# Mixture of experts: the sum over eight experts by identity matmuls on TensorE instead of reductions on VectorE

## The reference, cut to what matters

```
for e in range(E):                                   # E = 8 experts, 64 channels, 128 hidden
    h = gelu(einsum('bsd,dh->bsh', xn, W1[e]) + b1[e])
    y_e = einsum('bsh,hd->bsd', h, W2[e]) + b2[e]
    y = y + y_e * w_full[..., e, None]               # weights: softmax of the two largest logits, else 0
h = h + y
```

## Time and profile before

| | us |
|---|---|
| median of 3 runs (1759.25 to 1766.6) | 1764.92 |
| the profiled execution, its own time | 1765.77 |
| its span, first to last instruction | 1764.0 |
| TensorE busy | 1532.9 (87%) |
| VectorE busy | 1243.7 (71%) |
| ScalarE busy | 719.1 (41%) |
| POOL busy | 635.5 (36%) |
| mean granted clock of TensorE | 0.854 |

### The profile page before, as it was taken

The page is one execution under the profiler, slowest core; times in us unless marked ns, Lnnn a source line. Parts: engine busy times, 40 slices in busy tenths (PEclk is TensorE's granted clock), DMA queues, the critical chain, the costliest instruction groups (busy, mean ns, idle before and its releaser), DMA issues. The chain is left out here.

```text
span 1764.0 us, 46357 instructions
## 1 busy us (share of the span) xinstructions
PE 1532.9 (87%) x16040; PEld 1106.8 (63%) x16040; DVE 1243.7 (71%) x4135; ACT 719.1 (41%) x1908; POOL 635.5 (36%) x1142
## 2 busy tenths in 40 slices
PE   1299999999579999999999998379999997888887
PEld 1155566655346666666666665258888886777776
DVE  6136666666337788888888887566666665988887
ACT  2234444444145555555555554122222222444443
POOL 2624444444224445444454453321111122222220
PEclk9999999999689999999999998555555556988888
DMA  3000000000000000000000000000000000000000
GB/s 130 0 1 2 0 0 0 0 0 0 1 1 2 2 1 0 0 0 0 0 0 0 0 0 1 1 1 1 0 0 0 0 1 1 5 5 4 4 9 10
DMA packets 6981, 8.15 MB, mean 5 GB/s; under 512 B 6272, under 2 KB 6272, under 8 KB 6784
## 3 DMA queue, kind: packets, MB, share of 16 engines
q1 hardware_dynamic: 6912, 7.25, 1.2%
HBM read 5.71 MB, written 1.54 MB: 4 GB/s over the span
## 5 line engine op out<-in xcount | busy, mean ns | idle before, releaser
L1063 POOL TENSOR_SCALAR_AFFINE_SELECT ex_pT<-ex_pT 128x512 f32<-128x512 f32 (+1 forms) x256 | 127.0, 519 | 250.7 <-ACT ex_pT L1274 250.7
L1693 POOL TENSOR_TENSOR ta_kk<-ta_ext 94x320 f32<-94x320 f32 x64 | 60.4, 961 | 246.3 <-DVE ta_qkn L1873 162.9
L824 DVE RECIPROCAL al_rec<-al_O 128x188 f32<-128x188 f32 x64 | 85.0, 1329 | 58.7 <-PE al_O L668 58.7
L1332 DVE TENSOR_REDUCE ex_negmaxA<-ex_R 128x4 bf16<-128x512 f32 x128 | 88.2, 689 | 37.4 <-PE ex_R L1113 37.3
L564 POOL CAST al_kpadb<-al_kT 32x376 bf16<-32x376 f32 x128 | 63.0, 493 | 130.0 <-PE al_R L619 95.1
L1254 ACT ACTIVATE ex_pT<-ex_T 128x496 f32<-128x496 f32 x128 | 74.7, 583 | 86.2 <-PE ex_T L1151 85.1
L1053 POOL TENSOR_TENSOR ex_zrstd<-ex_zvar,neg_half 94x16 f32<-94x16 f32 x34 | 98.5, 2896 | 24.8 <-DVE ex_zvar L1441 24.8
L2062 PE MATMUL mo_H<-mo_xT,w_parts 128*128 128x188 bf16 x768 | 92.9, 281 | 8.9 <-ACT mo_hT L2102 8.9
L2102 ACT ACTIVATE mo_hT<-mo_H,wsb 128x188 f32<-128x188 f32 x256 | 88.1, 415 | 27.7 <-PE mo_H L2062 25.1
L725 ACT ACTIVATE al_pT<-al_T 128x496 f32<-128x496 f32 x128 | 74.4, 582 | 57.5 <-PE al_T L651 57.5
L2038 PE MATMUL mo_Y<-wsb,mo_hT 128*94 128x64 f32 x1024 | 94.9, 253 | 0.3 <-DVE mo_weighted L2161 0.3
(11 more groups left out here) (345 smaller groups left out, 4202.3 us busy)
## 6 DMA issues: line engine op xcount, KB each, us to landing
tok_xin<-x_t SPq DMA_DIRECT2D x4, 760.0 KB, 7.3
wsb<-weights SPq DMA_DIRECT2D x1, 2531.0 KB, 14.0
out<-stream SPq DMA_DIRECT2D x16, 94.0 KB
tok_par<-tok_w SPq DMA_DIRECT2D x1, 4.5 KB, 1.6
```

The source lines that it names most:

```text
L824: steps.link(nc.vector.reciprocal(rec[:], O[:, N:2 * N]))
L1063: nc.gpsimd.affine_select(out=view, in_=view, compare_op=ALU.is_ge, fill=0.0, base=shift, pattern=[[0, NH], [1, cols]], channel_multiplier ...
L1332: red(negmaxA[e % 2][:, D::32], R[:, 0, :].rearrange("p (n s) -> p n s", n=NH), AX.X, ALU.max, negate=True)\
```

## The change

The weighted outputs get a second buffer, and `mixed`, the result of the reductions, goes. TensorE gets a new group in its body, between L2046 and L2055: for sequence t-7, for each half, eight matmuls with the 94x94 identity as stationary operand and the weighted outputs of one expert (64 columns) as moving one, accumulated in PSUM, in columns 128 to 255 of the bank B2, whose columns 0 to 127 hold the gated biases. One increment of `b2_full`, after this group, now announces both. The bias matmuls wait for `sum_used`, the new group for `y_used`, `sum_used` and `b2_used`. VectorE's two reductions and their addition are replaced by one addition of the sum from PSUM to the stream, for sequence t-7, right after the addition of the biases.

```diff
-        weighted = sb("weighted", [P, HALVES, E, C])
-        mixed = sb("mixed", [P, HALVES, C])
+        weighted = two("weighted", [P, HALVES, E, C])
...
 # TensorE
                 if valid(r):
                     pe.wait_ge(gateT_ready, r + 1)
                     need(pe, b2_used, r)
+                    pe.wait_ge(sum_used, r + 1)
                     for h in range(HALVES):
                         last = nc.tensor.matmul(B2[0:P, h * C:(h + 1) * C], gateT[p][:, h * P:(h + 1) * P],
                                                 w("b2", E), start=True, stop=True)
+                r, p = t - 7, 1 - par
+                if valid(r):
+                    pe.wait_ge(y_used, HALVES * (r + 1))
+                    need(pe, sum_used, r)
+                    need(pe, b2_used, r - 1)
+                    for h in range(HALVES):
+                        for e in range(E):
+                            last = nc.tensor.matmul(B2[0:P, (HALVES + h) * C:(HALVES + h + 1) * C], ident[0:P, 0:P],
+                                                    weighted[p][:, h, e, :], start=(e == 0), stop=(e == E - 1))
+                if valid(t - 7) or valid(t - 8):
                     last.then_inc(b2_full, 1)
...
 # VectorE
                     for h in range(HALVES):
                         dve.wait_ge(y_full, HALVES * r + h + 1)
-                        nc.vector.tensor_tensor(weighted[:, h], YB[h][0:P, :].rearrange("p (e c) -> p e c", e=E),
+                        if valid(r - 2):
+                            dve.wait_ge(b2_full, r - 1)
+                        nc.vector.tensor_tensor(weighted[p][:, h], YB[h][0:P, :].rearrange("p (e c) -> p e c", e=E),
                                                 gate[p][:, h, :].unsqueeze(2).broadcast_to([P, E, C]), ALU.mult)\
                             .then_inc(y_used, 1)
                 r, p = t - 8, par
                 if valid(r):
-                    dve.wait_ge(b2_full, r + 1)
+                    dve.wait_ge(b2_full, r + 2)
...
-                r, p = t - 6, par
-                if valid(r):
-                    dve.wait_ge(y_used, HALVES * (r + 1))
-                    for h in range(HALVES):
-                        last = nc.vector.tensor_reduce(mixed[:, h, :], weighted[:, h].rearrange("p e c -> p c e"), AX.X, ALU.add)
-                    last.then_inc(mixed_set, 1)
-                    dve.wait_ge(mixed_set, r + 1)
-                    nc.vector.tensor_tensor(row_halves(r), row_halves(r), mixed[:], ALU.add).then_inc(stored, 1)
+                r, p = t - 7, 1 - par
+                if valid(r):
+                    dve.wait_ge(b2_full, r + 1)
+                    nc.vector.tensor_tensor(row_halves(r), row_halves(r),
+                                            B2[0:P, HALVES * C:2 * HALVES * C].rearrange("p (h c) -> p h c", h=HALVES),
+                                            ALU.add).then_inc(sum_used, 1)
```

More of the change, by code:

```diff
@@ L1968, in mixture @@
                  "h_full h_ready logits_full logits_set best_set behind_ready tanh_ready whichf_ready share_set "
-                 "pick_set gate_ready y_full y_used mixed_set gateT_full gateT_ready b2_full b2_used stored parts_ready fence").split()
+                 "pick_set gate_ready y_full y_used sum_used gateT_full gateT_ready b2_full b2_used stored parts_ready fence").split()
         (consts, stats_set, stats_settled, moments_ready, var_ready, rstd_ready, xn_set, xg_ready, xT_full, xT_ready,
          h_full, h_ready, logits_full, logits_set, best_set, behind_ready, tanh_ready, whichf_ready, share_set,
-         pick_set, gate_ready, y_full, y_used, mixed_set, gateT_full, gateT_ready, b2_full,
+         pick_set, gate_ready, y_full, y_used, sum_used, gateT_full, gateT_ready, b2_full,
          b2_used, stored, parts_ready, fence) = [ctx.enter_context(nc.semaphore("mo_" + n)) for n in names]
```

## The result

The changed kernel is slower, as forecast: 1800.13 us (median of 4, 1800.02 to 1802.98) against 1765.76 (4 runs then, 1759.25 to 1766.62). The ratio is 1.0207, with an interval of 1.018 to 1.0233. The forecast was 1805, the range 1790 to 1832. The profiled execution took 1802.98 us with a span of 1801.2; it is the slowest of the four, 2.9 us above the others. Its mean granted clock is 0.872 where theirs is 0.876, which makes an estimated 15 us more at half clock; only this execution has a trace, so where they lie is not known.

A forecast was written before the change was run, and what follows sets the result against it. VectorE was taken to set the 8.68 us step, TensorE close behind; with the identity group TensorE's step becomes 6.81 + 2.80 = 9.61 us. Steps summed to 1796.4, plus 7.3 of transfer a span of 1803.7; forecast 1805 us, range 1790 to 1832.

The forecast's parts named there:

- The bound and the slack: Mixture loop: VectorE sets the 8.68 us step; TensorE's own back-to-back step is 6.81, leaving 1.87 us of slack.
- What leaves VectorE: Mixture loop: 2.30 us a step of reductions and addition goes, 0.25 comes back; VectorE then needs 6.6 us.
- Some 3 us: Sign in the loop: VectorE idle that long a step, waiting for the second layer's products and the identity group.
- The price of the group: Identity group on TensorE: 32 instructions at second layer L2038's 87 ns, 2.80 us a row with waits.
- The step: Mixture loop: TensorE becomes the bound at 6.81 + 2.80 = 9.61 us, 0.93 longer than before.
- The waits: Added waits of bias matmul, identity group and VectorE's adds in the loop: all covered, cost nothing.
- the cover of 5 us: Mixture loop: VectorE's stretch to the logits read takes 4.6 us, TensorE needs it 9.61 after, so it is hidden.
- The sum: Whole mixture stage, steps added from 1493.74: last add ends at 1796.4, span 1803.7, forecast 1805 us.
- clock fall: Rival in the mixture stage: all at half clock, about 2010 us, 3%; occasional falls, 1826 to 1847 us, 8%.
- the rival's worry: Clock rival: busy TensorE does not assure 2.4 GHz; the Taylor stage's small float32 matmuls ran at 0.50, busy for 95%.
- The identity was not kept: Rival on the identity group: identity stays loaded over 16 matmuls, 1.03 us a row, total 1748 us; 3%.
- VectorE in the ring: Rival at the bias matmul's wait: VectorE's adds late each step, 0.6 to 1.0 us, total 1830 us; 4%.

The follow-up runs named there:

- e4_no_sum: Kernel before without the sum over the experts and its addition, left out of the output, nothing put on TensorE: 1715.47 us, ratio 0.9708.
- e3_wide: Changed kernel with both halves in one identity matmul, 8 of 128 columns a row in place of 16 of 64: 1770.44 us, ratio 1.0018.
- e1_keep_reduce: Changed kernel with the two reductions of each row put back on VectorE, their result unused: 1804.2 us, ratio 1.0217.
- e7_pool_sum: Kernel before with the sum over the experts on POOL as three additions of halves, nothing put on TensorE: 1753.71 us, ratio 0.9945.
- e6_quads: From e3_wide: VectorE first folds the products by two additions, then two identity matmuls of 128 columns a row on TensorE: 1737.84 us, ratio 0.9851.
- e8: e7_pool_sum with VectorE's addition of the sum moved from behind the weighting to ahead of it: 1751.11 us, ratio 0.9944.

## Why the prediction was right

Point by point, by its own steps:

- *The bound and the slack.* TensorE's own step of 6.81 us, read from one back-to-back step, was exact: e4_no_sum runs at 6.81. The slack of 1.87 us against a group of 2.8 was the whole argument, and it held.
- *What leaves VectorE.* VectorE was to need 6.6 us a step. After, it waits 2.54 for the identity group and about 0.2 for the second layer (4.4 us in 21 steps) in 9.48, so it needs 6.7. "Some 3 us" idle was 2.8.
- *The price of the group.* 2.80 forecast, 2.71 measured; e4 against the changed kernel gives 2.65 a row. The nearest row, L2038, was the right one to take. e3_wide fits: 64 more moving columns cost 29 ns, so some 56 of the 85 ns do not go with the moving columns, and L2038 has these 56 too. Both load 94 weight columns; that the 56 ns are the load was not tested by itself.
- *The step.* 9.61 forecast, 9.48 measured. 0.09 of the difference is the group (the 0.03 for its waits did not appear, and it takes 2.71 us where the logits follow it; where the transposed gates do, at 1777.64, it takes 2.81), 0.04 the logits' group, which starts its successor after 0.25 us and not 0.29.
- *The waits.* In the loop none showed on TensorE, as costed. e1_keep_reduce put 2.0 us a step of VectorE's work under the cover of 5 us and the step did not move. At the end of the kernel, where the steps are short, the cover is thin, and there e1 paid 3.8 of its 4 us.
- *The sum.* The first L2037 starts at 1493.98 (1493.74 forecast), the last bias and identity pair at 1787.85 (1791.05 and a wait of 0.7, 1791.75), the last addition ends at 1793.89 (1796.4), the span at 1801.2 (1803.7). The last pair is 3.9 us early. The 27 full steps give 3.1 of that: they took 256.35 us for 259.5, those of the loop 9.48 and the unrolled ones 9.54. The first two steps give 0.8, and 0.42 of it is a mistake in the sum: its first step of 6.34 us has transposed gates in it, and at that step no sequence has any yet. Behind the last pair the sum was 1.4 us too short: the identity group there takes 3.16 us and what follows it longer too, the clock falling to half at 1790.7, and the last bias matmul waits 0.41 us for ScalarE's copy of the gates, which the sum left out. The errors partly cancel, and that much of the small difference is luck. The profiled execution was forecast at 1805.5 and took 1802.98.
- *The rivals.* No clock fall from the first steps to 1790.7 us, where the kernel before had about one in every two steps. The gaps went with the change and the falls with them; in e7_pool_sum, where TensorE waits 16.3 us in 156 for the logits bank, the mean clock is 0.89 again. But not every gap brings a fall: in e6_quads TensorE waits 5.0 us in as long a window, never over 0.4 at a time, and the clock is 1.00 throughout. And the fall at 1790.7 came without a longer gap than 0.41 us, in the last identity group, when no hidden layer's matmul had run since 1774. So the rival's worry, that such matmuls by themselves do not hold the clock, is refuted for this stage with the hidden layer in every step, and not beyond it. The identity was not kept: its loads number 1024 more, one per instruction. VectorE in the ring: refuted by e1.

My forecast was 4.9 us too high in the median: 2.5 of it the span, 2.0 that this profiled execution stands 2.85 us above its median where I had taken over the 0.85 us of the one before, the rest rounding.

For the point on the clock, TensorE's waits for the logits bank in the window 1524 to 1680, e7's and then e6's (engine, what for: us in total, times, longest), and two windows at the end of the changed kernel, columns as in the earlier trace rows:
```profile
PE mo_LG L2070 <- DVE mo_logits L2155: 16.3, 15, 1.5
```
```profile
PE mo_LG L2066 <- DVE mo_logits L2151: 5.0, 17, 0.4
```
```profile
1786.00:1790.70 4.70, 4.29 (x49) 3.93 (x48) 0.48 (x2) 0.32 (x1) 0.00 (x0) 1.00 0.01 2
1790.70:1794.00 3.30, 2.47 (x15) 1.75 (x13) 0.77 (x3) 0.32 (x1) 0.00 (x0) 0.50 0.00 0
```

## What to carry to other kernels

Before moving work to another engine, measure that engine's step where it runs back to back, not its busy share: here 85% busy meant 1.87 us of slack a step, and the move needed 2.7. What is taken off the bound is worth no more than the distance to the next bound (50 us here, not the 60 of VectorE's own count), while what is put on that next bound counts in full. If a sum must go to TensorE by the identity, give each matmul more columns (128 in place of 64 brought 1800 us to 1770; wider was not tried), and fold by plain additions first (1738).

## What the runs showed of the hardware

- Float32 matmuls with the 94x94 identity as stationary operand: 85 ns an instruction with 64 moving columns, 114 ns with 128, two instructions and two loads for each matmul, also where the same identity follows itself 16 times. The Trainium skill (TensorE: Matmul & The Clock Gate, section "LDWEIGHTS (loading the stationary operand)") makes a load's time proportional to the weight columns, 78 ns for 94 as an estimate. The 85 ns are near that. But a load of 78 ns as the only bound does not fit the 114: at L2062's 0.505 ns a column, 64 and 128 columns are 32 and 65 ns, both under 78, and would cost the same. Measured are 29 ns for the 64 more columns, 0.45 each, on top of some 56 that stay. At half clock the instruction of 64 columns takes 165 ns (5.29 / 32), so its price goes with the clock, where the section's formula has no clock in it.
- TensorE held 2.4 GHz from 1500 to 1790 us at 96% busy with mostly float32 matmuls of 64 columns, while the stage before it, 95% busy, stood at 1.2 GHz. What tells the two apart was not tried.
- POOL's addition of two SBUF operands of 94x512 (1.26 us) holds up VectorE instructions on SBUF: an addition of two SBUF operands took 1375 ns for 289, normalizations 787 for 306, in e8 the multiplication of two SBUF operands behind them 700 for 288 beside POOL's next addition. An addition with one operand in PSUM, begun just before POOL's, kept its 0.28 us. The Trainium skill (SBUF — State Buffer, section "SBUF: two separate sides") says that VectorE and GpSimd share a port pair which one instruction holds to its end; the overlap in e7, where POOL's addition starts first and VectorE's ends 0.15 us after it, agrees.
